# Packed gate/up weights loaded across all partitions, and three steps of tile 1 and tile 2 set behind the four splits of y

## What is computed

```python
y  = x @ W.T + 2.0 * lora(x)                 # conditioning, 512 -> 512
wq = (qweight_gu >> 4*r) & 15                # eight 4-bit values in a word, along the rows
w_gu = scale[g] * (wq - (zq[g] + 1))         # 512 x 2752: gate and up, 1376 columns each
inter = y @ w_gu
gate, up = inter[..., :1376], inter[..., 1376:]
h = silu(gate) * up
x = x + h @ dequant(down)
```

## Time and profile before

| | |
|---|---|
| median of three runs | 440.8 us (440.32 to 441.22) |
| the profiled execution | 441.64 us, of which the span of the instructions is 439.8 us |
| busy share of the span | PE 99%, DVE 76%, ACT 51%, POOL 48% |
| granted TensorE clock | full (2.4 GHz) in all 40 slices |
| chain of work that ended last | PE 89%, DMA 4%, DVE 3%, POOL 2% |

### The profile page before, as it was taken

One profiled execution on the slowest core, in us unless ns is written; L12 is line 12 of the kernel. 1 busy time (PEld: TensorE's weight loads), 2 busy tenths in 40 slices (PEclk: granted clock), 3 DMA queues, 4 the chain that ended last, 5 costly groups with the idle time before them and its releaser, 6 DMA issues.

```text
span 439.8 us, 5493 instructions
## 1 busy us (share of the span) xinstructions
PE 434.9 (99%) x1938; PEld 355.0 (81%) x1938; DVE 333.4 (76%) x413; ACT 223.6 (51%) x301; POOL 210.9 (48%) x182
## 2 busy tenths in 40 slices
PE   8999999999999999999999999999999999999997
PEld 4788787888888888888888888888888888888886
DVE  3968999889888854746778578878687678999922
ACT  4505575665555344245677756466465554474200
POOL 0368987879887403300014787996987300000000
PEclk9999999999999999999999999999999999999999
DMA  8955124301225466575289427848569136986623
GB/s 267 228 175 178 51 74 145 86 26 19 25 24 136 128 222 256 243 284 191 97 270 371 173 84 237 296 136 261 181 214 301 56 121 262 364 281 183 224 98 143
DMA packets 29401, 78.20 MB, mean 178 GB/s; under 512 B 2432, under 2 KB 15888, under 8 KB 27712
## 3 DMA queue, kind: packets, MB, share of 16 engines
q1 hardware_dynamic: 25312, 66.07, 43.9%
q0 software_dynamic: 3488, 11.10, 9.7%
q10 hardware_dynamic: 576, 0.72, 0.5%
HBM read 57.15 MB, written 20.73 MB: 177 GB/s over the span
## 4 chain that ended last, share of the span: by engine, by line
PE 89%; DMA 4%; DVE 3%; POOL 2%; issue 1%; SPq 0%; ACT 0%; DVEq 0%
PE ps L1938 10%; PE ps L1940 10%; PE ps L1939 10%; PE ps L1806 7%; PE ps L1808 6%; PE ps L1807 6%; PE ps L1683 6%; PE ps L1684 6%; PE ps L1687 6%; PE ps L2053 5%; PE ps L2051 5%; PE ps L2052 5%; DMA res<-in_xT 2%; PE ps L1921 2%; PE ps L1919 2%; PE ps L1920 2%
## 5 line engine op out<-in xcount | busy, mean ns | idle before, releaser
L1938 PE MATMUL ps<-zt_hi,ring_hi 128*128 128x512 f32 x140 | 54.6, 390 | 0.0
L1939 PE MATMUL ps<-zt_lo,ring_hi 128*128 128x512 f32 x140 | 54.5, 389 | 0.0
L1940 PE MATMUL ps<-zt_hi,ring_lo 128*128 128x512 f32 x140 | 54.5, 389 | 0.0
L761 ACT ACTIVATE ring_hi<-raw 128x1792 fp32r<-128x1792 f32 (+2 forms) x32 | 38.7, 1238 | 23.8 <-PE ps L1940 10.1
L1122 DVE TENSOR_TENSOR ring_lo<-raw,ring_hi 128x1024 fp32r<-128x1024 f32 (+3 forms) x24 | 41.4, 1730 | 6.9 <-ACT ring_hi L761 6.9
L1683 PE MATMUL ps<-h_hi,d_hi 128*128 128x512 f32 x88 | 34.2, 389 | 0.0
L1684 PE MATMUL ps<-h_lo,d_hi 128*128 128x512 f32 x88 | 34.2, 389 | 0.0
L671 POOL TENSOR_TENSOR raw<-raw 128x256 f32<-128x256 f32 x21 | 25.4, 1209 | 15.1 <-DMA raw<-in_gu 11.0
L1938 PEld LDWEIGHTS ps<-zt_hi,ring_hi 128*128 128x128 f32 x140 | 26.3, 188 | 5.9 <-issue 0.4
L633 POOL DMA_INDIRECT scale<-in_sc_gu,idx_gu x20 | 28.0, 1401 | 5.8 <-issue 5.8
L1940 PEld LDWEIGHTS ps<-zt_hi,ring_lo 128*128 128x128 f32 x140 | 26.3, 188 | 5.5
(11 more groups left out here) (254 smaller groups left out, 1189.1 us busy)
## 6 DMA issues: line engine op xcount, KB each, us to landing
ad_raw<-in_w1T SPq DMA_DIRECT2D x8, 1024.0 KB, 4.9
wd<-down_weights SPq DMA_DIRECT2D x7, 1024.0 KB, 5.7
down_weights<-dhi SPq DMA_DIRECT2D x7, 896.0 KB, 4.6
down_weights<-dlo SPq DMA_DIRECT2D x7, 896.0 KB, 4.1
raw<-in_gu SPq DMA_DIRECT2D x12, 512.0 KB, 3.6
wd<-down_weights SPq DMA_DIRECT2D x7, 768.0 KB, 5.6
draw<-in_d SPq DMA_DIRECT2D x7, 512.0 KB, 4.8
res<-in_xT SPq DMA_DIRECT2D x1, 2048.0 KB, 7.8
```

Source lines behind the costliest of these rows:

```text
L1938: pe.matmul(ps[:, bank, :], ring1_hi[s][:, w], z_hi[:, t], start=first and k == 0, stop=False, skip_group_check=True)
L1939: pe.matmul(ps[:, bank, :], ring1_hi[s][:, w], z_lo[:, t], start=False, stop=False, skip_group_check=True)
L1940: ins = pe.matmul(ps[:, bank, :], ring1_lo[s][:, w], z_hi[:, t], start=False, stop=k == 1, skip_group_check=True)
```

## The change

It has two parts.

The packed weights are still loaded by two DMAs of SyncE. Before, each brought all eleven tiles to 64 partitions, and both read the same array of 64 rows. Now the array has 128 rows (the 64 rows twice), the first DMA brings tiles 0 to 4 to all 128 partitions and the second tiles 5 to 10. Bytes moved stay the same. The wait (`s_qw` at 32, for both) stays too.

Three steps move to another place: `w_hi(1)` on ScalarE, `w_lo(1)` and `dequant_gu(2)` on VectorE.

```diff
-            for hp in range(2):
-                sp.dma_start(nib[64 * hp:64 * hp + 64, :].bitcast(U32), a["qw_gu"]).then_inc(s_qw, 16)
+            for i0, i1 in NIB_PARTS:
+                c = slice(2 * P * i0, 2 * P * i1)
+                sp.dma_start(nib[:, c].bitcast(U32), a["qw_gu"][:, c]).then_inc(s_qw, 16)
...
             w_hi(0)
             y_split(0, 0)
-            w_hi(1)
             y_split(1, 4)
             y_copy(0, 0, 1)
             y_copy(1, 4, 2)
             y_split(2, 6)
             y_split(3, 2)
+            w_hi(1)
             y_copy(3, 2, KD)
...
             w_lo(0)
             y_split(0, 0)
-            w_lo(1)
             y_split(1, 4)
             add_zeros(1)
-            dequant_gu(2)
             y_split(2, 6)
             y_split(3, 2)
+            dequant_gu(2)
+            w_lo(1)
             dequant_gu(3)
             add_zeros(2)
```

More of the change, by code:

```diff
@@ L235, in build @@
         ident = cst[:, C_ID:C_ID + P]
+        NIB_PARTS = ((0, 5), (5, FT0))
         ZERO_PARTS = ((0, 2), (2, 5), (5, FT0))
@@ L1211, in _ @@
             lo(b_lo[:, :], b_raw[:, :], b_hi[:, :], s_wlo0)
-            NIB_PARTS = ((0, 5), (5, FT0))
             def nibbles(part):
@@ L2156 @@
         "bT": v["L0_cond_B"].transpose(0, 2, 1).reshape(E * R, D)[:, order],
-        "qw_gu": np.ascontiguousarray(qg.transpose(0, 2, 1, 3)).view(np.uint8).reshape(64, FT0, 2 * P, 4).transpose(0, 1, 3, 2).reshape(64, -1).view(np.uint32),
+        "qw_gu": np.tile(np.ascontiguousarray(qg.transpose(0, 2, 1, 3)).view(np.uint8).reshape(64, FT0, 2 * P, 4).transpose(0, 1, 3, 2).reshape(64, -1), (2, 1)).view(np.uint32),
         "sc_gu": sc_rows[:2 * NPAIRS].reshape(NPAIRS, 2, G_GU, 2 * P).transpose(0, 2, 1, 3).reshape(NPAIRS * G_GU, 4 * P),
```

## The result

| | before | changed |
|---|---|---|
| median | 441.08 us (440.32 to 443.0, 8 runs) | 443.96 us (443.36 to 444.49, 8 runs) |
| ratio | | 1.0065, 95% interval 1.0053 to 1.0077 |
| span of the profiled execution | 439.8 us | 442.7 us |

The account below looks back on a forecast made before the run. PE was taken as the bound, with VectorE deciding at product 4 of tile 2. VectorE's earlier scaling (-0.2) and POOL collisions (+1.0) gave +0.8 us on a median of 440.8: 441.6 us, range 439.7 to 442.7.

Parts of the forecast that it names:

- The load: Packed-weight DMAs to 128 partitions: end 2.7 us earlier, so POOL's gathers and VectorE's start come up to 2.7 us earlier.
- VectorE up to 60 us: VectorE's row after the reorder: block 3 low part ends at 44.5, scaling of tile 3 starts near 46.8, additions collide.
- the sum for `y_c_22(2)`: VectorE's step that PE awaits at product 4 of tile 2: 0.8 us later, ready at 75.5.
- term for the collisions: POOL's eight additions of tiles 2 and 3 all collide with VectorE's SBUF work: 1.0 us more, at most 1.4.
- a shift taken at 74.86 stays as it is to the end: After product 4 of tile 2, VectorE has idle time again from 77.47, so PE's delay neither grows nor shrinks.
- the base: Median of the kernel before, 440.8 us, 0.84 below the profiled execution; the +0.8 us was added to it.
- The gain of 1.25 us: PE's first gap, at 44.8 before the third row block of gate 0, goes: 1.25 us gained at that place.
- (a): PE keeps its 1.25 us because `y_c_22` is early enough at product 4 of tile 2: 439.55 us, chance 18%.
- the listed wait: PE's 1.0 us wait for a low part of y, in gate 0, forecast to vanish.
- (b): Collisions of POOL's additions with VectorE do not grow: shift -0.2 us, 440.6 us, chance 17%.
- (c): The load is no faster, block 3 of y is ready at 45.8, VectorE 1.25 us later still: 442.85 us, chance 10%.
- the 1.25 us gained at 44.8 are given back: PE waits about 2 us before product 4 of tile 2, losing the 1.25 us and 0.8 more.

Follow-up runs that it names:

- kernel 1: The new load alone, with the old order on VectorE and ScalarE, against the kernel before: 440.66 us, ratio 0.9999.
- kernel 5: The changed kernel with POOL's additions of tiles 4 and 5 cut to 4 of 128 columns: 441.90 us, ratio to the kernel before 1.0033.
- kernel 6: The changed kernel with POOL's sums of tiles 4 and 5 waiting for VectorE's low parts of tiles 3 and 4: 442.13 us, ratio to before 1.0023.
- kernel 2: The new order alone, with the old load to 64 partitions twice, against the kernel before: 444.30 us, ratio 1.0093.

## Why the prediction was wrong

**The load** was right in its direction and too small in size, which did no harm. POOL waits 0.30 us ("issue") instead of 3.23 before its first `zg` gather, as it does in kernel 1 and in the second profile of the changed kernel. The later load came about 7 us earlier and not 2.7: before, it was issued at 6.9 and landed 16.8 us later, now both have landed by 16.4. VectorE's first scaling starts at 31.63, 4.0 us earlier, where 33 was forecast. The Trainium skill ("SBUF — State Buffer", section "Door 1: The DMA port swizzle") says that a load to partitions 0 to 63 reaches half of the ports that one to all 128 partitions reaches. The rates agree with that, 221 GB/s against 410; its 328 GB/s for 128 partitions at 1 MiB was exceeded here, and the 2.9 us worked out from its figures fell short.

**VectorE up to 60 us** was right nearly to a tenth. Block 3's low part was forecast to end at 44.5 (41.90 + 2.59 = 44.49), the scaling of tile 3 to start near 46.8 (46.84), POOL's last sum of tile 3 to end near 59.8 (59.65). All eight additions collided with VectorE's SBUF work (none took less than 1.53 us). The product of silu and up starts at 60.66, against 60.02 in the first profile: +0.64 where the sum had +0.8.

One row was misread on the way: the addition at 47.06 does not run while VectorE reads PSUM. The two that do are those at 45.67 and 46.37. VectorE has begun the scaling of tile 3 at 46.94, and the additions of 46.37 and 47.06 end only at 47.11 and 47.80: the 0.7 us that the scaling lost are the rest of one addition and the whole of the next. So this row already shows VectorE waiting past the end of one addition, where the sum took 0.7 us as the most that one addition can cost.

**The first step that failed** is the sum for `y_c_22(2)`, "-0.2 + 1.0 = +0.8 us", in its term for the collisions. I counted only the additions of tiles 2 and 3 and took what follows at its old durations. But POOL, no longer waiting for VectorE before the sums of tile 4, now ran them exactly when VectorE began the low part of tile 3: 2.23 us against 1.28 before. `y_c_22(2)` ended at 76.31, +0.64 + 0.95 = +1.6 instead of +0.8. The runs without these additions (kernel 5) and with them set back (kernel 6) had a low part of tile 3 of 0.95 and 0.94 us and came within 1.25 and 0.74 us of the kernel before.

**The second** is "a shift taken at 74.86 stays as it is to the end". Idle time on VectorE after 77.47 was no proof of that, because the shift between POOL and VectorE was new as well. The low part of tile 4 took 2.95 us for 0.96, and PE lost another 0.8 us at product 4 of tile 3, in one of two profiles; 0.3 us more went at 105 us. In sum 1.6 + 0.8 + 0.3 = 2.7 of the 2.9 us between the two first profiles. The last 0.3 us is not the change's: the second profile of before has the same wait, at 102 us.

**The third** is the base. I added +0.8 us, worked out against an execution of 441.64 us, to a median that was 0.84 us lower. That takes for granted that the median execution has the same gap. The second profile shows one of 440.36 us without it. The gain of 1.25 us, which the sum set against VectorE's delay, exists only in some executions; the order was to be judged against VectorE's slack of 1.06 us and not against a gap. How many executions of the kernel before have the gap was not measured; its times spread over 2.0 us on the chip of kernel 1 (25 runs, 440.00 to 441.98), where the kernel with the new load and the old order spread over 1.2 us (12 runs, 440.05 to 441.25).

**The rivals.** The gain that stays (a) did not come: the listed wait vanished and VectorE decided, as argued. The growing collisions were real, against (b). The slower side (c) was the right sign by the wrong mechanism: the load was faster, and the loss came from the turns between POOL and VectorE. Even with the old load (kernel 2) block 3 of y was not late. The step "the 1.25 us gained at 44.8 are given back" held: PE is ahead by 1.4 us at 62 us and has lost it at 76.

What stays open is the rule by which POOL's additions follow each other while VectorE waits. At the low part of tile 3 VectorE got its turn after one addition in the first profile of before, where it started 0.27 us behind that addition, and after two in the changed kernel, 0.07 us behind; at the low part of tile 4 it got it after three, 0.02 us behind. In the changed kernel both turns came at the end of POOL's third addition (70.87 and 81.20), ahead of the 0.15 us pause that POOL makes before its fourth. Why no turn came sooner is not shown.

## What to carry to other kernels

An instruction count and a list of waits don't show slack: profile a second execution before building on a gap of 1 us, and ask of each engine how much idle time it has ahead of the place where another waits for it. Costs of moves need not add up. Here one move fitted into 1 us of slack, the other went over it by about 1 us, and together they cost three times that. And when POOL and VectorE both work on SBUF, a step set back on VectorE also sets back what POOL does for it, so the times at which the two meet must be followed for several stages, or be tied by a wait: kernel 6 came from a ratio of 1.0065 to 1.0023 with a wait and no other change, though the same idea one stage earlier (the sums of tile 3) gained nothing in five of six executions, because the time it freed went into a longer wait and a lower clock.

## What was not expected of the hardware

A two-operand VectorE instruction waited not for one GpSimd addition but for up to three in a row (2.95 us for 0.96, 3.02 for 1.21), and with the two starts 0.01 to 0.02 us apart it waited for none in one execution and for three in another. After 2.19 us without a matmul PE ran on at half rate, the lower of its two levels (1.2 GHz): from the third on, seven matmuls take 0.43 us each from start to start instead of 0.23, with 0.60 of the clock granted in the window of 75 to 79 us. After 1.37 us without one, in the changed kernel, the granted clock stayed at 1.00. The seven slow matmuls cost 1.4 us, more than half of what the wait itself did.
